# A four-layer graph network on one core: layers 1 and 2 worked by batches, biases by a row of ones, a shorter norm, and a counting ladder in PSUM

## The chip, the core and the metric

The kernel runs on one core of a Trainium2 chip. The metric is the device time of one execution in microseconds (us); lower is better. The engines are TensorE (PE; its weight loads are listed as PEld), VectorE (DVE), ScalarE (ACT), GpSimd (POOL) and SyncE (SP). POOL here issues all indirect DMAs (gathers, scatters and scatter-adds by index), SP and ACT the plain ones.

## What is computed

A graph of 3125 nodes with 64 features and 100000 edges, sorted by destination, goes through four layers. Each is `x = x + layer(relu(layernorm(x)))`, the norm without gain and bias.

```python
edge_index = jnp.stack([src, dst])
h = jnp.maximum(_layernorm(x, axis=-1), 0.0)
x = x + _L0_gnn_ref(h, edge_index, edge_weight, edge_weight_n2, ...)   # signed similarity, sums over dst and src
h = jnp.maximum(_layernorm(x, axis=-1), 0.0)
x = x + _L1_gnn_ref(h, edge_index, edge_type_8, ...)                   # 8 relations of attention
h = jnp.maximum(_layernorm(x, axis=-1), 0.0)
x = x + _L2_gnn_ref(h, src, dst, ...)                                  # gated messages, sum and max
h = jnp.maximum(_layernorm(x, axis=-1), 0.0)
x = x + _L3_gnn_ref(h, edge_index, ...)                                # 4 heads, batch norms, MLP
```

In layer 1 a node gets, besides the sum over its edges, its own row: `x @ W_self + b_self`, and for each relation r `alpha_self[r] * (h @ W[r]) + bias[r]` (the self loop). In layer 2 an edge takes `relu([h[src], h[dst]] @ We1 + be1)`, which the kernel splits in two tables: one row for the source and one for the destination, the latter with the bias `be1`.

## The kernel before

The nodes lie on 125 partitions with 25 tiles of 64 features each (`xn` is x, `hn` the normed h, `agg` what was collected, all 128x25x64 float32); node work goes in NBATCH = 5 batches of NB = 5 tiles. The edges lie on 128 partitions with 784 columns in 98 groups of 8. The five engines run their own hand-written programs and meet by counting semaphores; each takes its instructions strictly in the order in which they are written. The arena is one large SBUF tile whose parts have many names in the code.

**Layer 0.** POOL adds 784 columns of edge weights one by one into a table in DRAM, `weights0` (`add0`, line 707), in 14 windows of 56 columns. Beside this DVE merges equal keys (`merge_window`), norms x (`norm_relu(0)`), makes tables, and counts the edges of each node: `one_hot` (line 1536) compares, for a group of 8 columns, the row 0, 1, 2, ... (`iota_row`, the ladder, an SBUF tile) with the place of each edge, once 8x128 and once 8x25 wide, into bfloat16 ones and zeros; PE multiplies these (line 1118) and DVE adds the 25 counts (line 1529). That is 98 rounds. Then 32 tiles are weighed and summed (`weigh0`, `bend0`, `similarity0`, lines 1615, 1625 and 1633), each as soon as SP could load its cells (line 547), which waits for all windows of adds that the tile needs. The last three tiles need the last window.

**Between layers 1 and 2.** When the states of the edges are in DRAM (`state1`), POOL runs `whole_segments` and then `collect` twice (line 694): 25 gathers of `betas` (16 numbers a node) into `beta_n`, and 25 gathers of `state1` into `agg`. All count up one semaphore, `agg_in`; in the first collection POOL waits after each five until these have landed. DVE's `nodes1b` takes a batch: two small instructions on `beta_n`, then the products of PE (`mix`, line 1066: 5 narrow ones with `W_self`, 5 wide ones with the eight relations) in two parts, tiles 0 to 2 and 3 to 4 (`parts`). In a part DVE multiplies by the weights (line 1864, out of PSUM), sums over the eight relations with a reduction over a strided view (line 1866) and adds to `xn` (line 1868); the first part also adds the own product and the bias row (lines 1862 and 1863). Only when all five batches and all 25 gathers of `state1` are done, DVE adds `agg` to all of `xn` (line 1872), runs `norm_relu(2)` over all 25 tiles (lines 1477 to 1487; ACT takes the root, line 831), and begins `nodes2`.

**`nodes2`** goes by batches: DVE stages five tiles of `hn` (line 1492), PE transposes them (line 1052), ACT copies the result to `hT` (line 840), PE multiplies (line 1066, 5 products of 256 columns), and DVE copies one half to `tb2` (line 1883), `hn` beside it (line 1884), and the other half plus the bias `be1` to `bn_rows` (line 1886). SP stores `tb2` (line 581). After each batch POOL scatters its five tiles of `bn_rows` to `put2` (`put`, line 663); after the last it waits until they have landed, does `hold` (line 668), and begins the 784 gathers of layer 2 (`gather`, line 674).

## Time and profile before

| | us |
|---|---|
| median of 3 runs | 5234.94 |
| lowest and highest | 5234.36, 5235.63 |
| the profiled execution | 5238.84 |
| its span, in which all rows are placed | 5236.9 |

All starts and stretches below are in us from the start of that span. The profiled execution is 3.9 us above the median; 1.9 us of it lie around the span. The page puts DVE at 75% busy, POOL at 68%, PE at 54% and ACT at 15%: no engine is busy throughout, so what counts is who is waited for in each stage. A row of a timeline has the start, the busy time, engine, line, operation, output and inputs, how many, and in brackets the idle time before it with what ended it. A row of a grouped list has count, total busy time and mean of one, then the idle time of the engine just before.

### The profile page before, as it was taken

The page shows a single profiled execution, that of the slowest core. Times are in us where ns is not written, and L with a number is a line of the kernel's source. Part 1 is how long each engine was busy: PE and PEld are TensorE (multiplying, and loading weights), DVE is VectorE, ACT ScalarE, POOL GpSimd, SP SyncE. Part 2 cuts the span into 40 slices and gives each one's busy share as a digit, 9 for nine tenths or more (in the row PEclk, how much of TensorE's full clock was granted, in tenths as well). Part 3 has the DMA queues.
Part 4 walks back from the last instruction along what each step waited for, and adds up shares of the span by engine and source line. Part 5 has one row for each costly group of instructions (what it writes and reads, how often), then busy time and mean ns, then how long its engine had stood idle before and what let it go on. Part 6 is the DMA issues. An engine that isn't in the chain of part 4 may idle for free.

```text
span 5236.9 us, 62187 instructions
## 1 busy us (share of the span) xinstructions
PE 2819.4 (54%) x10695; PEld 1383.4 (26%) x10695; DVE 3951.2 (75%) x10482; ACT 777.7 (15%) x1979; POOL 3567.1 (68%) x3644
## 2 busy tenths in 40 slices
PE   5844277326675000014555555555777777738993
PEld 4522122104665000012222222222333333313332
DVE  8866999436999986655777777744888888889993
ACT  0000032110000025530222222210000000003331
POOL 4777777753777877755777777754777777725552
PEclk9999987657999555556777777667999999969996
DMA  9320266313444368852556656635999999938990
GB/s 348 139 89 9 76 228 225 126 63 123 165 159 159 122 234 301 298 182 88 182 179 183 181 180 179 182 96 204 307 309 313 308 311 308 311 123 285 332 324 21
DMA packets 458404, 1041.74 MB, mean 199 GB/s; under 512 B 129581, under 2 KB 247829, under 8 KB 427884
## 3 DMA queue, kind: packets, MB, share of 16 engines
q1 hardware_dynamic: 167018, 580.42, 30.8%
q0 software_dynamic: 131968, 217.09, 15.0%
q10 hardware_dynamic: 159234, 242.47, 13.3%
q14 instruction: 154, 1.26, 0.1%
q8 instruction: 30, 0.49, 0.0%
HBM read 560.07 MB, written 477.20 MB: 198 GB/s over the span
## 4 chain that ended last, share of the span: by engine, by line
POOL 43%; issue 20%; PE 16%; DVE 11%; DMA 7%; ACT 1%; DVEq 1%; POOLq 0%; ACTq 0%; SPq 0%
POOL arena L674 25%; POOL weights L707 16%; PE psum L1232 5%; PE psum L1233 4%; DMA arena<-tab,ring 4%; PE psum L1283 3%; DVE arena L2086 1%; DVE arena L1574 1%; DVE arena L1833 1%; PE psum L1066 1%; POOL agg L694 1%; DVE arena L2015 1%; POOL arena L694 1%; ACT arena L962 1%; DVE arena L1921 1%
## 5 line engine op out<-in xcount | busy, mean ns | idle before, releaser
L674 POOL DMA_INDIRECT arena<-tab,ring x2352 | 2313.4, 984 | 717.4 <-issue 697.0
L1232 PE MATMUL psum<-arena,ident 128*128 128x512 f32 x1176 | 791.3, 762 | 720.9 <-DMA arena<-tab,ring 537.2
L1574 DVE SCALAR_TENSOR_TENSOR arena<-arena,ns 128x64 f32<-128x64 f32 (+2 forms) x2351 | 870.1, 370 | 274.4 <-issue 74.8
L707 POOL DMA_INDIRECT weights<-arena x784 | 832.1, 1061 | 293.0 <-issue 238.7
L1233 PE MATMUL psum<-arena,ident 128*128 128x512 f32 x1176 | 723.0, 702 | 0.0
L1232 PEld LDWEIGHTS psum<-arena,ident 128*128 128x128 f32 x1176 | 265.0, 241 | 1142.7 <-issue 606.3
L777 POOL TENSOR_TENSOR arena<-arena,score 128x256 f32<-128x256 f32 x294 | 230.6, 809 | 256.8 <-issue 123.0
L1283 PE MATMUL psum<-arena,ident 128*128 128x512 f32 x784 | 362.8, 609 | 63.9 <-DVE arena L2086 63.8
L2015 DVE SCALAR_TENSOR_TENSOR arena<-psum,rowb 128x1024 f32<-128x1024 f32 x196 | 239.1, 1220 | 197.6 <-PE psum L1233 196.9
L1233 PEld LDWEIGHTS psum<-arena,ident 128*128 128x128 f32 x1176 | 271.7, 231 | 382.5 <-issue 382.5
L1154 PE MATMUL psum<-arena 64*128 64x400 f32 x512 | 159.4, 709 | 273.1 <-DVE arena L1633 265.1
L1200 PE MATMUL psum<-agg,arena 128*128 128x200 bf16 x2352 | 236.7, 250 | 118.7 <-DVE arena L1691 118.0
L1700 DVE SCALAR_TENSOR_TENSOR arena<-iota_row,base,psum 128x200 f32<-128x200 f32 x784 | 283.1, 417 | 1.6 <-PE psum L1200 1.6
L2086 DVE TENSOR_TENSOR arena<-arena,score 128x256 f32<-128x256 f32 x490 | 244.7, 538 | 28.0 <-PE psum L1283 27.9
L2022 DVE TENSOR_REDUCE arena<-arena 128x8 f32<-128x512 f32 x392 | 265.0, 677 | 0.1
L1900 DVE SCALAR_TENSOR_TENSOR arena<-psum,rowb 128x1024 f32<-128x1024 f32 x98 | 119.8, 1223 | 179.5 <-PE psum L1233 179.5
L1406 DVE SCALAR_TENSOR_TENSOR arena<-psum,arena,upper 128x128 bf16<-128x128 f32 x784 | 227.5, 348 | 30.6 <-PE psum L1023 30.1
L1083 PE MATMUL psum<-ident,arena 128*64 128x128 f32 (+1 forms) x3 | 1.2, 405 | 460.7 <-DVEq L1745 452.4
L1615 DVE SCALAR_TENSOR_TENSOR arena<-arena,limit 128x800 f32<-128x800 f32 x128 | 133.6, 1044 | 143.0 <-DMA arena<-weights 143.0
L1200 PEld LDWEIGHTS psum<-agg,arena 128*128 128x128 bf16 x2352 | 191.4, 98 | 152.1 <-DVE arena L1700 80.1
L897 ACT ACTIVATE arena<-arena,score 128x64 f32<-128x64 f32 x784 | 197.6, 334 | 211.2 <-DVE arena L1574 150.1
L1921 DVE SCALAR_TENSOR_TENSOR arena<-arena,ns 128x64 f32<-128x64 f32 x783 | 217.6, 278 | 6.3 <-ACT arena L962 4.8
(388 smaller groups left out, 4152.3 us busy)
## 6 DMA issues: line engine op xcount, KB each, us to landing
put<-zero SPq DMA_DIRECT2D x98, 1040.0 KB
arena<-put SPq DMA_DIRECT2D x98, 1040.0 KB, 7.5
spill<-arena ACTq DMA_DIRECT2D x98, 1024.0 KB, 5.4
arena<-spill SPq DMA_DIRECT2D x98, 1024.0 KB
state<-arena ACTq DMA_DIRECT2D x147, 512.0 KB, 3.6
weights<-zero SPq DMA_DIRECT2D x32, 1600.0 KB, 18.3
arena<-weights SPq DMA_DIRECT2D x32, 1600.0 KB, 7.5
put<-zero SPq DMA_DIRECT2D x14, 3584.0 KB
```

What stands on the lines that cost most here:

```text
L674: pool.indirect_dma_start(out=rows[:, h, k, :], out_offset=None, in_=table[:, :], in_offset=bass.IndirectOffsetOnAxis(ap=ring[:, h, word + ...
L707: pool.indirect_dma_start(out=weights0[:, :], out_offset=bass.IndirectOffsetOnAxis(ap=words0[:, g, k:k + 1], axis=0), in_=words0f[:, g, K ...
L1200: mm = pe.matmul(bank(2 + 2 * h + k // 2)[:, k % 2 * NT * R:(k % 2 + 1) * NT * R], lhsT=picks[:, h, k, :], rhs=s_parts[:, a, :], start=(a ...
L1232: pe.matmul(place, lhsT=ident[:, :], rhs=rows_of[0][:, s, columns, 0:width], start=True, stop=False)
L1233: mm = pe.matmul(place, lhsT=ident[:, :], rhs=rows_of[1][:, s, columns, 0:width], start=False, stop=True)
L1283: mm = pe.matmul(bank(h).rearrange("p (c k) -> p k c", k=K), lhsT=ident[:, :], rhs=y3[:, h, :, head * D:(head + 1) * D], start=(head == 0) ...
L1574: beats.add(dve.scalar_tensor_tensor(out=rows[:, s, k, :], in0=before, scalar=mark(ns, g, k), in1=rows[:, s, k, :], op0=ALU.mult, op1=ALU. ...
L1700: pick = dve.scalar_tensor_tensor(out=sifted[:, h * 4 + k, :], in0=iota_row[:, :], scalar=src_column[:, column], in1=bank(2 + 2 * h + k // ...
L1921: scans2.add(dve.scalar_tensor_tensor(out=st2[:, h, k, 0:D], in0=zero[:, 0:D] if start else prior[:, 0:D], scalar=mark(ns, g, k), in1=m2[: ...
L2015: beats3.add(dve.scalar_tensor_tensor(out=pr3[:, columns, :], in0=bank(4 * h + 2 * part, 2).rearrange("p (k c) -> p k c", c=HD), scalar=0. ...
L2022: beats3.add(dve.tensor_reduce(rs3[:, columns, :], pr3[:, columns, :].rearrange("p k (h c) -> p k h c", c=D), AX.X, ALU.add))
L2086: makes3.add(dve.tensor_tensor(y3[:, s % 2, k, :].rearrange("p (h c) -> p h c", c=D), gc3[:, s, k, 0:HD].rearrange("p (h c) -> p h c", c=D ...
```

## The change

1. **The counting ladder.** DVE copies the first 128 numbers of `iota_row` to PSUM bank 7 once, and `one_hot` reads them there. Its output and other input stay in SBUF.
2. **The norm.** The mean's scaling goes into the subtraction, epsilon and the scaling of the variance into ACT's root (bias and scale), and the relu into the last multiplication: eight DVE instructions become six.
3. **Biases.** A row of ones is added to `hT` (65th row), and `b_self` plus the eight relation biases, and `be1`, are written to the 65th row of the weights. The additions of the biases in `nodes1b` and `nodes2` go. The eight additions that form the bias go from between layers 1 and 2 to layer 0, before the weighing.
4. **Collecting.** POOL issues the 50 gathers of both collections one after the other; each batch has its own semaphore (`loops_in`, `arrived`).
5. **The sum over relations** is three additions (of 4, 2 and 1 rows) in place of the strided reduction.
6. **Add, norm and multiply by batches.** DVE adds `agg`, norms and stages a batch (`arrive1`) before the products of the batch ahead of it are copied out. ACT takes part in copying: tiles 2 and 3 (`ends2`), DVE the others.
7. Loops over the batches are written out, and some semaphores (`rows_in`, `kept`) are shared between stages with higher counts.

The core of the diff:

```diff
+            tally.done(pool.memset(hT_full[D:D + 1, :, :], 1.0), consts)
+            def collect_batches(table, index, rows, landed):
+                for i in range(NT):
+                    pool.indirect_dma_start(out=rows[:, i, :], out_offset=None, in_=table[:, :],
+                                            in_offset=bass.IndirectOffsetOnAxis(ap=index[:, i:i + 1], axis=0)).then_inc(landed[i // NB], 16)
-            collect(1, betas, eidx, beta_n, before=0)
-            ready((agg_in, 16 * NT))
-            collect(1, state1, eidx, agg)
+            collect_batches(betas, eidx, beta_n, loops_in)
+            collect_batches(state1, eidx, agg, arrived)
...
-                ready((taken, 15 + b + 1))
+                ready((rows_up, b + 1), (taken, 15 + b + 1))
...
-            deviation(2)
-            lift_only(3)
+            def ends2(b):
+                act.wait_ge(mixed, 15 + b + 1)
+                act.wait_ge(tab_out, b * 16 + 16 * (1 + 1 * NBATCH))
+                halves = bank(1).rearrange("p (j c) -> p j c", c=2 * HID)
+                act.activation(bn_rows[:, bass.ds(b * NB + 2, 2), :], halves[:, :, HID:2 * HID], ACT.Copy)
+                act.activation(tb2[:, 2:4, 0:HID], halves[:, :, 0:HID], ACT.Copy).then_inc(rows_up, 1)
+            for b in range(NBATCH):
+                deviation_of(2 + b, b)
+                if b:
+                    ends2(b - 1)
+                lift(3, b)
+            ends2(NBATCH - 1)
...
+            ladder = bank(7)[:, 0:P]
+            step(dve.tensor_copy(ladder, iota_row[:, 0:P]))
-                    dve.tensor_tensor(hots[:, h * K:h * K + K, :], spread(iota_row[:, 0:width].unsqueeze(1), P, K, width),
+                    dve.tensor_tensor(hots[:, h * K:h * K + K, :], spread(ladder[:, 0:width].unsqueeze(1), P, K, width),
...
+            def norm_batch(use, b):
+                at = bass.ds(b * NB, NB)
+                col = [lnv[:, k, at] for k in range(4)]
+                step(dve.tensor_reduce(col[0], xn[:, at, :], AX.X, ALU.add))
+                step(dve.scalar_tensor_tensor(out=hn[:, at, :], in0=spread(col[0].unsqueeze(2), P, NB, D), scalar=-1.0 / D, in1=xn[:, at, :],
+                                              op0=ALU.mult, op1=ALU.add))
+                step(dve.tensor_tensor(agg[:, at, :], hn[:, at, :], hn[:, at, :], ALU.mult))
+                step(dve.tensor_reduce(col[1], agg[:, at, :], AX.X, ALU.add))
+                dve.sem_inc(root_in, 1)
+                dve.wait_ge(root_out, use + 1)
+                step(dve.reciprocal(col[3], col[2]))
+                step(dve.scalar_tensor_tensor(out=hn[:, at, :], in0=hn[:, at, :], scalar=0.0, in1=spread(col[3].unsqueeze(2), P, NB, D),
+                                              op0=ALU.max, op1=ALU.mult))
...
-                        beats1n.done(dve.tensor_tensor(xn[:, at, :], xn[:, at, :], spread(row["b_self"].unsqueeze(1), P, NB, D), ALU.add))
-                    beats1n.done(dve.tensor_reduce(red1[:, lo:hi, :], prod1[:, lo:hi, :, :].rearrange("p j r c -> p j c r"), AX.X, ALU.add))
+                    for rows in (4, 2):
+                        beats1n.done(dve.tensor_tensor(prod1[:, lo:hi, 0:rows, :], prod1[:, lo:hi, 0:rows, :], prod1[:, lo:hi, rows:2 * rows, :], ALU.add))
+                    beats1n.done(dve.tensor_tensor(red1[:, lo:hi, :], prod1[:, lo:hi, 0, :], prod1[:, lo:hi, 1, :], ALU.add))
...
-            step(dve.tensor_tensor(xn[:, :, :], xn[:, :, :], agg[:, :, :], ALU.add))
-            norm_relu(2)
+            def arrive1(b):
+                at = bass.ds(b * NB, NB)
+                dve.wait_ge(arrived[b], 16 * NB)
+                step(dve.tensor_tensor(xn[:, at, :], xn[:, at, :], agg[:, at, :], ALU.add))
+                norm_batch(2 + b, b)
+                stage(3, b, hn)
...
+            arrive1(0)
+            for b in range(NBATCH):
+                if b < NBATCH - 1:
+                    arrive1(b + 1)
+                nodes2(b)
```

POOL's program at the two collections, from the end of `whole_segments` to the first scatter of layer 2; before:

```order
L694 DMA arena<-betas,eidx 128x16 [waits open_moved,beta_out]
L694 DMA arena<-betas,eidx 128x16 x4
L694 DMA arena<-betas,eidx 128x16 [waits agg_in]
L694 DMA arena<-betas,eidx 128x16 x4
...
L694 DMA agg<-state,eidx 128x64 [waits agg_in]
L694 DMA agg<-state,eidx 128x64 x24
L663 DMA put<-arena,zidx 103552x128 [waits taken]
```

and now:

```order
L695 DMA arena<-betas,eidx 128x16 [waits open_moved,beta_out]
L695 DMA arena<-betas,eidx 128x16 x24
L695 DMA agg<-state,eidx 128x64 x25
L667 DMA put<-arena,zidx 103552x128 [waits rows_up,taken]
L667 DMA put<-arena,zidx 103552x128 x4
```

The five waits of POOL on landed gathers are gone, and the scatter waits for two semaphores in place of one.

DVE's program from the end of `nodes1b` to the first copies of layer 2, where `lnv` holds the sums and roots of the norm and `hst` the staged batch; before:

```order
L1872 TENSOR_TENSOR xn<-xn,agg 128x1600 [waits agg_in,taken]
L1477 TENSOR_REDUCE lnv<-xn 128x25 [waits vec]
L1478 TENSOR_SCALAR lnv<-lnv 128x25 [waits vec]
L1479 TENSOR_TENSOR hn<-xn,lnv 128x1600 [waits vec]
L1480 TENSOR_TENSOR agg<-hn 128x1600 [waits vec]
L1481 TENSOR_REDUCE lnv<-agg 128x25 [waits vec]
L1482 TENSOR_SCALAR lnv<-lnv 128x25 [waits vec]
L1485 RECIPROCAL lnv<-lnv 128x25 [waits vec,root_out]
L1486 TENSOR_TENSOR hn<-hn,lnv 128x1600 [waits vec]
L1487 TENSOR_SCALAR hn<-hn 128x1600 [waits vec]
L1492 TENSOR_SCALAR hst<-hn 128x320 [waits turned,vec]
...
L1883 COPY arena<-psum 128x5x128 [waits tab_out,mixed]
```

and now:

```order
L1933 TENSOR_TENSOR xn<-xn,agg 128x320 [waits arrived0,taken]
L1520 TENSOR_REDUCE lnv<-xn 128x5 [waits vec]
L1521 SCALAR_TENSOR_TENSOR hn<-lnv,xn 128x320 [waits vec]
L1523 TENSOR_TENSOR agg<-hn 128x320 [waits vec]
L1524 TENSOR_REDUCE lnv<-agg 128x5 [waits vec]
L1527 RECIPROCAL lnv<-lnv 128x5 [waits vec,root_out]
L1528 SCALAR_TENSOR_TENSOR hn<-hn,lnv 128x320 [waits vec]
L1534 TENSOR_SCALAR hst<-hn 128x320 [waits turned,vec]
L1933 TENSOR_TENSOR xn<-xn,agg 128x320 [waits arrived1]
...
L1940 TENSOR_SCALAR arena<-hn 128x5x64 [waits tab_out]
L1945 COPY arena<-psum 128x256 [waits mixed,node_vec3]
```

Eight instructions on 320 columns now stand between `nodes1b` and the first staged batch, and the same eight for batch 1 stand ahead of the copies of batch 0.

## Rows read from the trace of the kernel before

**Rows 1.** The page's part 4: the chain that ended last, by line.

```profile
POOL arena L674 25%; POOL weights L707 16%; PE psum L1232 5%; PE psum L1233 4%; DMA arena<-tab,ring 4%; PE psum L1283 3%; DVE arena L2086 1%; DVE arena L1574 1%; DVE arena L1833 1%; PE psum L1066 1%; POOL agg L694 1%; DVE arena L2015 1%; POOL arena L694 1%; ACT arena L962 1%; DVE arena L1921 1%
```

**Rows 2.** Groups by line and shape, window 500 to 632, then 30 to 333, then 632 to 1143.

```profile
L1536 DVE TENSOR_TENSOR arena<-iota_row,arena 128x1024 bf16<-128x1024 f32 x81 | 98.2, 1212 | 0.0
L707 POOL DMA_INDIRECT weights<-arena x82 | 98.0, 1196 | 25.0 <-issue 25.0
...
L707 POOL DMA_INDIRECT weights<-arena x215 | 206.4, 960 | 119.5 <-issue 65.3 <-DVE arena L1428 54.3
...
L707 POOL DMA_INDIRECT weights<-arena x368 | 402.0, 1092 | 112.2 <-issue 112.2
...
L1615 DVE SCALAR_TENSOR_TENSOR arena<-arena,limit 128x800 f32<-128x800 f32 x116 | 121.1, 1044 | 93.7 <-DMA arena<-weights 93.7
```

**Rows 3.** Timeline around 540, DVE and POOL, two rounds of the counting.

```profile
540.14 1.49 DVE L1536 TENSOR_TENSOR arena<-iota_row,arena 128x1024 bf16<-128x1024 f32 x2
...
540.99 1.20 POOL L707 DMA_INDIRECT weights<-arena  x1 [0.30 <-issue]
```

**Rows 4.** Stretch 475 to 622: busy us (x instructions) of each engine, PEclk, DMA share, GB/s.

```profile
475.00:622.00 147.00, 38.34 (x784) 28.53 (x784) 146.53 (x294) 0.00 (x0) 117.24 (x98) 1.00 0.02 2
```

**Rows 5.** Timeline around 707, DVE and POOL, in the weighing of tiles.

```profile
706.74 0.99 DVE L1633 TENSOR_TENSOR arena<-arena,psum 128x800 f32<-128x800 f32 x1
706.85 0.96 POOL L707 DMA_INDIRECT weights<-arena  x1 [0.30 <-issue]
707.64 1.05 DVE L1615 SCALAR_TENSOR_TENSOR arena<-arena,limit 128x800 f32<-128x800 f32 x1
...
708.12 1.40 POOL L707 DMA_INDIRECT weights<-arena  x1 [0.30 <-issue]
```

**Rows 6.** Timeline: the last scatter-add, and the first weighing after it.

```profile
1142.63 0.96 POOL L707 DMA_INDIRECT weights<-arena  x1 [0.30 <-issue]
...
1152.02 1.05 DVE L1615 SCALAR_TENSOR_TENSOR arena<-arena,limit 128x800 f32<-128x800 f32 x1 [49.31 <-DMA arena<-weights]
```

**Rows 7.** Timeline, POOL's collections: first gather, first after a wait, last.

```profile
2326.81 0.96 POOL L694 DMA_INDIRECT arena<-betas,eidx  x1 [2.11 <-DMA state<-open_sum,open_end]
...
2334.86 0.95 POOL L694 DMA_INDIRECT arena<-betas,eidx  x1 [2.10 <-DMA arena<-betas,eidx]
...
2397.37 0.94 POOL L694 DMA_INDIRECT agg<-state,eidx  x1 [0.30 <-issue]
```

**Rows 8.** Timeline, DVE in `nodes1b`, first part of batch 1.

```profile
2348.51 0.49 DVE L1862 TENSOR_TENSOR xn<-xn,psum 128x320 f32 x1 [3.31 <-PE psum L1066]
2349.03 0.49 DVE L1863 TENSOR_TENSOR xn<-xn,rowb 128x320 f32 x1
...
2351.35 2.73 DVE L1866 TENSOR_REDUCE arena<-arena 128x192 f32<-128x1536 f32 x1
```

**Rows 9.** Timeline, DVE from the collected sums to the staged batch.

```profile
2399.86 1.83 DVE L1872 TENSOR_TENSOR xn<-xn,agg 128x1600 f32<-128x1600 f32 x1 [4.03 <-DMA agg<-state,eidx]
...
2409.36 0.18 DVE L1482 TENSOR_SCALAR lnv<-lnv 128x25 f32<-128x25 f32 x1
2409.89 0.31 DVE L1485 RECIPROCAL lnv<-lnv 128x25 f32<-128x25 f32 x1 [0.35 <-ACT lnv L831]
...
2413.12 0.33 DVE L1492 TENSOR_SCALAR hst<-hn 128x320 f32<-128x320 f32 x1
```

**Rows 10.** Timeline, batches of `nodes2`: PE, DVE, and POOL's scatters.

```profile
2415.62 4.50 PE L1066 MATMUL psum<-we_sb,hT 128*128 128x256 f32 x10 [0.79 <-ACT hT L840]
...
2420.16 0.82 DVE L1883 COPY arena<-psum 128x640 f32<-128x640 f32 x1 [4.96 <-PE psum L1066]
...
2423.10 1.00 POOL L663 DMA_INDIRECT put<-arena,zidx  x1 [24.78 <-DVE arena L1886]
...
2453.45 0.96 POOL L663 DMA_INDIRECT put<-arena,zidx  x1 [0.30 <-issue]
```

**Rows 11.** Timeline, DVE: the relu of the norm at layers 1 and 3.

```profile
1222.51 0.99 DVE L1487 TENSOR_SCALAR hn<-hn 128x1600 f32<-128x1600 f32 x1
...
3552.50 0.99 DVE L1487 TENSOR_SCALAR hn<-hn 128x1600 f32<-128x1600 f32 x1
```

More of the change, by code:

```diff
@@ L364, in gnn_program @@
         agg_in = sem("agg_in")
+        loops_in, arrived = ([sem(f"{name}{b}") for b in range(NBATCH)] for name in ("loops_in", "arrived"))
+        rows_up = sem("rows_up")
         result_out = sem("result_out")
@@ L1608, in _ @@
                 tally.done(dve.tensor_reduce(folded[:, :, :], prod.rearrange("p a (h c) -> p a h c", c=D), AX.X, ALU.add), wa_set)
+            dve.wait_ge(consts, 20)
+            for r in range(R):
+                step(dve.tensor_tensor(row["b_self"], row["b_self"], row["bias_rel"][:, r * D:(r + 1) * D], ALU.add))
+            for weights, bias in ((wself_full[D:D + 1, :], row["b_self"][D:D + 1, :]), (we1_full[D:D + 1, 1, :], row["be1"][D:D + 1, :])):
+                tally.done(dve.tensor_copy(weights, bias), wa_set)
             def weigh0(at, c):
@@ L1846, in _ @@
             dve.sem_inc(ended, 1)
-            for r in range(R):
-                step(dve.tensor_tensor(row["b_self"], row["b_self"], row["bias_rel"][:, r * D:(r + 1) * D], ALU.add))
-            beats1n = Beats(dve, node_vec[2], 8)
+            beats1n = Beats(dve, node_vec[2], 11)
             def nodes1b(b):
```

102 lines of the change are left out of this document (58 added, 44 removed).

## The prediction

> **What bounds the kernel now.** I read the chain that ended last first, since no engine is busy throughout. By line it belongs above all to POOL: 25% of the span are gathers of line 674 and 16% the scatter-adds of line 707 [rows 1]. The change touches neither loop of gathers, so I looked at the two places where it meets the chain: the scatter-adds, which run until 1143, and the stretch between layers 1 and 2, from 2327 to about 2455. For each I read the groups of instructions by stage and then the timeline.
>
> **Scatter-adds.** POOL waits there for nothing but its own issue, 0.30 us apiece, so its time per add is the length of the issue. Undisturbed one lasts 0.96 us (215 of them before 333), but 1.20 while DVE counts, and 1.09 on average while tiles are weighed [rows 2]. The timeline tells why. In the weighing, line 1615 reads two operands in SBUF: it ran from 707.64 to 708.69, and the add that began at 708.12 ended at 709.52, 0.83 after it. An add beside line 1633, whose second operand is in PSUM, took its 0.96 [rows 5]. In the counting DVE's line 1536 also reads two SBUF operands and the add that began at 540.99 took 1.20 [rows 3]: the 1024-wide comparison of 1.21 us began at 540.14 and ended at 541.35, and the add ended 0.84 after it. The two loops are locked: in 147 us there are 294 instructions of DVE (98 rounds of three) and just 98 issues of POOL, 1.50 us each [rows 4]. DVE itself is busy all the time and is not slowed.
>
> **Between the layers.** POOL begins the collections at 2326.81, waits after each five gathers (8.05 us for five), and issues the last at 2397.37 [rows 7]. DVE had sat idle for 4.03 us when that had landed; then it adds and norms all 25 tiles, from 2399.86 to 2413.12 [rows 9]. PE's first products last from 2415.62 to 2420.1, and POOL, idle for 24.78 us, begins to scatter at 2423.10. Its 25 scatters then follow one another: the last is at 2453.45, so 24 steps are 30.35 us, 1.26 each, with no room between [rows 10]. DVE's and PE's later batches are hidden behind them. So what counts is when the first scatter can start, and whether the others can still follow at 1.26.
>
> **The change, part by part.**
>
> *Ladder in PSUM.* The comparison then has one operand in SBUF, as line 1633 has, and an add beside it should take 0.96, so that 98 issues cost 1.26 in place of 1.50: 98 x 0.24 = **23.5 us**. What is late next? DVE keeps its 147 us for the counting (a comparison of PSUM with SBUF costs per element what one of two SBUF tiles costs: 0.99 us for 800, where 1024 of the present kind take 1.21, both 1.2 ns each [rows 2, 5]), so it is DVE that ends the counting, and POOL leaves it with 19 more adds done. The adds in the weighing are still stretched: 368 x 0.13 = 48 us for 116 instructions of line 1615, 0.41 each [rows 2], and these tiles are the same after the change. When the last add was out, DVE had been idle for 49.31 us [rows 6]; a last add 23.5 earlier finds it idle still. The eight bias additions and two copies now ahead of the weighing (some 2.5 us of DVE) fall into the same idle time. The lower bound is zero, if the stall has another cause; the upper is about 28, should the stretching in the weighing fall by a tenth with another phase.
>
> *Collections without waits.* 50 x 1.25 = 62.5 us from 2326.81: the last issue is at 2388.1 and has landed near 2391, 9 us earlier. DVE's new additions of two SBUF operands will stretch some of these issues. By the same reckoning a DVE instruction of length L costs a chance issue L x L / 2.5: 0.4 for the widest (below, 0.98), some 0.8 a batch in all, 4 us. That puts the last landing near 2395, which the norm of batch 4 needs only at about 2415. Hidden.
>
> *Sum over relations, and bias.* First part of a batch: the bias addition goes (0.52), and the reduction (2.76 with its gap [rows 8]) becomes additions of 768, 384 and 192 numbers. An addition takes 1.05 ns a number and 0.17 with its gap (0.49 for 320 and 1.83 for 1600 [rows 8, 9]): 0.98 + 0.57 + 0.37 = 1.92. Saved: 0.84 + 0.52 = 1.36. PE's next products start only when DVE has released the part, and DVE waits for them (3.31 us in batch 1), so this saving lies on the cycle of every batch: 5 x 1.36 = 6.8. The second part (1024 columns) saves 0.4 once, at the end. DVE was done 4.03 us before 2399.86, at 2395.8; now at 2388.6, and 2388.9 with some delay by POOL.
>
> *Norm by batches.* On 320 columns: four instructions of 0.51 (add, reduce, square, reduce), two of 0.53, 0.38 for ACT's root and 0.2 for the reciprocal: 3.7 us, where all 25 tiles took 13.3. Staged at 2392.6. From there as before: 2.5 to the products (2413.12 to 2415.62), 4.5 for them, and then four copies of DVE from PSUM with ACT's two beside them, 1.4 in place of 2.1, and 0.85 until POOL's scatter: 2.3. First scatter: 2392.6 + 2.5 + 4.5 + 2.3 = 2401.9, against 2423.10: **-21.2 us**.
>
> *Do the others follow?* DVE's cycle is now 4.0 (norm and staging of the next batch) + 0.45 (`hn` beside) + 1.4 (copies) = 5.9, with some delay by POOL 6.2, against 6.3 for five scatters. DVE's four instructions with two SBUF operands stretch POOL's issues by 4 x 0.1 a batch over four batches: +1.7. A PE that takes 4.5 for each batch is still ahead of DVE, since it works during the norm. So the last scatter comes at 2401.9 + 30.4 + 1.7 = 2434.0, **-19.4 us**. Bounds: -23 if PE's products run at their faster pace and nothing is stretched; -14 if DVE's cycle is 8 us, so that it, not POOL, sets the pace (2401.9 + 4 x 8 + 5.1 = 2439).
>
> *Shorter norm.* Two small instructions of 0.18 (0.22 and 0.27 with gap and signal) and the relu (1.03) go, and two instructions grow by 0.05: 1.4 us. In layers 1 and 3 nothing runs beside it [rows 11]: **2 x 1.4 = 2.8 us**. In layer 0 it is hidden by the adds.
>
> *At nothing:* loops written out, semaphores shared (each wait has its old meaning), the row of ones (one more memset of POOL, in the 54.3 us in which its first add waits for DVE [rows 2]). Between zero and 1 us either way.
>
> **Sum:** 23.5 + 19.4 + 2.8 = 45.7. Against the profiled execution, 5238.8 - 45.7 = 5193.1; the median lies 3.9 lower, so I forecast **5189** for it.
>
> **A rule of the Trainium skill.** The rows say that an add waits for a DVE instruction with two SBUF operands and not for one with an operand in PSUM. "SBUF — State Buffer", section "Who interferes with whom", has a rule for this (a DVE instruction with two SBUF inputs contends with a GpSimd instruction that reads SBUF), and by it the whole 23.5 us come. The same section infers that `tensor_tensor` does not hold up descriptors, as writing these needs the write interface; by that sentence the ladder's move would bring nothing. Rows 5 speak for the first.
>
> **Rivals.**
> *Ladder for nothing.* The comparison would still hold POOL, by its other operand or its bfloat16 output. For it: no row shows this very instruction with a PSUM operand. Against it: lines 1633 and 1615 differ in just that [rows 5]. Then the sum is 22.2: 5213. Chance 0.08.
> *DVE sets the pace of the scatters.* Each batch of DVE's has some 13 small instructions with waits between, two handovers to ACT, and POOL in its way. With a cycle of 8 us the time is 5 more: 5194. Chance 0.15.
> *Slower than before: reading the ladder from PSUM is slow.* A row of 128 numbers is read eight times over, 98 times. If a round took x us longer, DVE would begin the weighing 98x later. It idles there for 93.7 us before 1143 and for 49.3 at the end [rows 2, 6], 143 in all, of which POOL's lead takes 23.5; so up to x = 1.2 nothing is lost. From there DVE ends the layer, and the time is 5235 - 22 - 143 + 98x: above 5235 from x = 1.7, more than a doubled round, and 5286 at x = 2.2. The rows of line 1633 give x near 0. Chance 0.01.
> *Lead lost.* Something else than POOL ends layer 0 some 10 us later than I think, or a stage after it gives time back: 5199. Chance 0.06.
>
> **How the numbers follow.** Forecast as it stands, within some 3 us: 0.70, at 5189. The range of 8 in 10 takes in the slower pace, the lost lead and the upper ends (28, 23 and 3 make 54, which is 5181): 5181 to 5203. Beyond it lie the ladder for nothing and the slow ladder. A measurement of this kernel can tell about 0.2% (10 us) from no change. Every case but the slow ladder is faster by more than that: faster 0.97, same 0.02, slower 0.01.
>
> **What would show it.** Right: the adds of line 707 during the counting near 0.96 with more than 110 issues in the stretch; the last add near 1119; a first scatter of layer 2 some 21 us, and a last one some 19 us, earlier relative to the first gather of `betas`; the distance of scatters 1.26 to 1.35. Wrong: adds of 1.20 beside the counting; counting rounds longer than 1.5; gaps of DVE in POOL's scatters; DVE no longer idle before the last tiles of layer 0.

## The result, and the profile after

| | before | changed |
|---|---|---|
| median of 4 runs each, us | 5234.65 (5233.18 to 5235.63) | 5184.68 (5178.88 to 5186.93) |
| ratio to before | 1 | 0.9903 (95%: 0.9886 to 0.9920) |
| profiled execution, its span, us | 5238.84, 5236.9 | 5185.38, 5183.7 |
| last scatter-add, us of the span | 1142.63 | 1116.24 |
| first gather of `betas` | 2326.81 | 2298.14 |
| first, last scatter between layers 1 and 2 | 2423.10, 2453.45 | 2370.57, 2401.59 |

The changed kernel is 50 us (0.97%) faster. The forecast was 5189 us in a range from 5181 to 5203; the median lies 4.3 us below it, inside the range but outside the 3 us that I had given a chance of 0.70. The span is 53.2 us shorter, and the four places in the table divide it: 26.4 by the last add, 2.3 from there to the first gather, 23.2 between the layers, and 1.3 behind them.

**The counting.** The timeline of the changed kernel around 537 (columns as in [rows 3]), then its groups by line and shape in the window 500 to 632, as in [rows 2], and its stretch 475 to 622, as in [rows 4]:

```profile
537.27 1.48 DVE L1582 TENSOR_TENSOR arena<-psum,arena 128x1024 bf16<-128x1024 f32 x2
537.40 0.96 POOL L717 DMA_INDIRECT weights<-arena  x1 [0.31 <-issue]
538.66 0.96 POOL L717 DMA_INDIRECT weights<-arena  x1 [0.30 <-issue]
```

```profile
L717 POOL DMA_INDIRECT weights<-arena x101 | 98.0, 971 | 30.8 <-issue 30.8
L1582 DVE TENSOR_TENSOR arena<-psum,arena 128x1024 bf16<-128x1024 f32 x80 | 97.1, 1214 | 0.0
```

```profile
475.00:622.00 147.00, 39.76 (x787) 29.74 (x783) 145.68 (x296) 0.00 (x0) 111.33 (x118) 1.00 0.03 2
```

The comparison now has PSUM as its first input and lasts what it lasted (1214 ns against 1212). An add that runs wholly beside it takes 0.96 where [rows 3] have 1.20. In the same 147 us DVE makes 296 instructions (294 before), and POOL 118 issues in place of 98: the lock of one issue to a round is gone. Seven issues of each count are not adds but gathers of `tab` (line 668, now 672), which the prediction had taken with the adds; they fell from 1196 to 952 ns each, so gathers are held up like adds.

**The last add** (as in [rows 6]): DVE still idles 47.37 us behind it for the next tile, so POOL, not DVE, ends layer 0.

```profile
1116.24 0.96 POOL L717 DMA_INDIRECT weights<-arena  x1 [0.31 <-issue]
...
1125.45 1.05 DVE L1666 SCALAR_TENSOR_TENSOR arena<-arena,limit 128x800 f32<-128x800 f32 x1 [47.37 <-DMA arena<-weights]
```

**Between the layers.** Timeline of DVE in `nodes1b`, first part of batch 0 ([rows 8] show batch 1, which now begins at 2318.10 and has the same instructions); the three additions that replace the reduction of 2.73 us take 2308.37 to 2310.38, and the bias addition behind line 1911 is gone:

```profile
2306.06 0.49 DVE L1911 TENSOR_TENSOR xn<-xn,psum 128x320 f32<-128x320 f32 x1
2306.58 1.76 DVE L1912 TENSOR_TENSOR arena<-psum,arena 128x1536 f32<-128x1536 f32 x1
2308.37 1.61 DVE L1915 TENSOR_TENSOR arena<-arena 128x768 f32<-128x768 f32 x2
2310.02 0.36 DVE L1916 TENSOR_TENSOR arena<-arena 128x192 f32<-128x192 f32 x1
```

Then the sum and norm of batch 0, its products and the scatters (answering to [rows 9, 10]; DVE, PE and POOL):

```profile
2357.25 0.49 DVE L1933 TENSOR_TENSOR xn<-xn,agg 128x320 f32<-128x320 f32 x1
...
2360.26 0.19 DVE L1527 RECIPROCAL lnv<-lnv 128x5 f32<-128x5 f32 x1 [0.42 <-ACT lnv L845]
...
2361.00 0.52 DVE L1534 TENSOR_SCALAR hst<-hn 128x320 f32<-128x320 f32 x1
...
2363.71 4.63 PE L1090 MATMUL psum<-we_sb,hT 128*128 128x256 f32 x10 [0.79 <-ACT hT L854]
...
2368.45 0.42 DVE L1945 COPY arena<-psum 128x256 f32<-128x256 f32 x1 [2.54 <-PE psum L1090]
...
2370.57 1.00 POOL L667 DMA_INDIRECT put<-arena,zidx  x1 [7.83 <-DVE arena L1949]
...
2401.59 0.96 POOL L667 DMA_INDIRECT put<-arena,zidx  x1 [0.30 <-issue]
```

From the addition to the staged batch it is 3.75 us, where all 25 tiles took 13.3 (the norm itself now has six DVE instructions where it had nine, not eight as said under "The change"). POOL waits 7.83 us for its first scatter in place of 24.78. The last gather is issued at 2361.68, after the norm of batch 0 has begun.

### The profile page after: what moved, and what is told of

Read it like the earlier page. It is cut to its first block, busy times and chain, and to the rows that moved or that the text cites. A ratio compares the mean times of both kernels' runs of the same rounds, so it can differ in the third digit from the quotient of the medians.

```text
span 5183.7 us, 62148 instructions
## 1 busy us (share of the span) xinstructions
PE 2812.5 (54%) x10695; PEld 1380.3 (27%) x10695; DVE 3938.8 (76%) x10527; ACT 782.5 (15%) x1993; POOL 3545.7 (68%) x3645
## 4 chain that ended last, share of the span: by engine, by line
POOL 50%; issue 21%; PE 13%; DVE 10%; DMA 5%; DVEq 1%; POOLq 1%; ACT 0%; ACTq 0%; SPq 0%
POOL arena L678 33%; POOL weights L717 16%; PE psum L1311 3%; PE psum L1260 3%; PE psum L1261 3%; DMA arena<-tab,ring 3%; PE psum L1090 2%; DVE arena L2152 1%; DVE arena L1884 1%; DVE arena L1620 1%; DVE arena L2081 1%; DVE arena L1769 1%; POOL agg L704 0%; DVE arena L2132 0%; POOL arena L704 0%
## 5 line engine op out<-in xcount | busy, mean ns | idle before, releaser
L717 POOL DMA_INDIRECT weights<-arena x784 | 807.0, 1029 | 292.7 <-issue 238.7
L1666 DVE SCALAR_TENSOR_TENSOR arena<-arena,limit 128x800 f32<-128x800 f32 x128 | 133.5, 1043 | 115.7 <-DMA arena<-weights 115.7
```

The lines of the kernel that those rows point to most:

```text
L717: pool.indirect_dma_start(out=weights0[:, :], out_offset=bass.IndirectOffsetOnAxis(ap=words0[:, g, k:k + 1], axis=0), in_=words0f[:, g, K ...
```

## The experiments

The theory on record with the runs (**A**): POOL's issue of an indirect DMA is held up while DVE runs an instruction with two operands in SBUF, and not while one of them is in PSUM; POOL's issues set the end of layer 0. The rival **B**: the comparison holds POOL anyway (by its bfloat16 output, or by what it is), and the gain comes from the layers behind. For the second half: what the batches of the norm are worth, against the cheaper sum and biases alone. Unless another is named, each experiment is compared with the kernel before on its own chip. On the chip of the first four runs that one takes 5246.64 us.

**1. The ladder alone.** The kernel before, with only this:

```diff
+            ladder = bank(7)[:, 0:P]
+            step(dve.tensor_copy(ladder, iota_row[:, 0:P]))
...
-spread(iota_row[:, 0:width].unsqueeze(1), P, K, width)
+spread(ladder[:, 0:width].unsqueeze(1), P, K, width)
```

> The kernel before with only the ladder of the counting in PSUM. Theory A (a scatter-add waits for a DVE instruction with two SBUF operands): adds beside the counting take 0.96 us, about 117 issues in 475 to 622 instead of 98, and the kernel is 23.4 us (0.45%) faster. Theory B (the gain before the last add comes from the shorter norm or from DVE's order): adds stay at 1.20 and the time within 5 us.

Measured: 5219.76 us, ratio 0.9949 (0.9932 to 0.9966), 26.9 us less. Its groups in the window 500 to 615:

```profile
L1539 DVE TENSOR_TENSOR arena<-psum,arena 128x1024 bf16<-128x1024 f32 x78 | 94.3, 1210 | 0.0
L707 POOL DMA_INDIRECT weights<-arena x89 | 85.2, 958 | 27.1 <-issue 27.1
```

One operand moved and nothing else, and the issue is 958 ns: A.

**2. The other operand.** The kernel before with the ladder left in SBUF and the places it is compared with in PSUM. This asks whether it is PSUM as the ladder's home that matters, or the number of operands in SBUF.

```diff
+            pn_up, im_up = bank(4, 2)[:, 0:T], bank(6, 2)[:, 0:T]
+            step(dve.tensor_copy(pn_up, pn))
+            step(dve.tensor_copy(im_up, im))
...
-for hots, place, width in ((hot_p, pn, P), (hot_i, im, NT)):
+for hots, place, width in ((hot_p, pn_up, P), (hot_i, im_up, NT)):
```

> The kernel before with the ladder left in SBUF, but the other operand, the places of the edges, copied to PSUM (four banks, two copies of 784 columns, some 2 us of DVE). Theory A1 (what counts is that one of two operands is not in SBUF, whichever): the same gain as with the ladder in PSUM, 20 to 24 us. Theory A2 (it is the ladder's read, the same 128 numbers eight times over, or the tile that all of them share): no gain, within 3 us.

Measured: 5223.15 us, ratio 0.9955 (0.9938 to 0.9972), 23.5 less. Window 500 to 615:

```profile
L1540 DVE TENSOR_TENSOR arena<-iota_row,psum 128x1024 bf16<-128x1024 f32 x77 | 92.9, 1206 | 0.0
L707 POOL DMA_INDIRECT weights<-arena x89 | 85.5, 961 | 27.1 <-issue 27.1
```

Either operand will do. The output is still bfloat16 in SBUF, so writing it is not what holds POOL here.

**3. The ladder back.** The changed kernel with line 1582 reading `iota_row` in SBUF again (the diff of experiment 1, backwards).

> The changed kernel with the ladder back in SBUF. Theory A: 23.4 us slower than the changed one, adds of 1.20 beside the counting, last add near 1140, some 26 us faster than the kernel before. Theory B: within 5 us of the changed kernel.

Measured: 5223.63 us, ratio 0.9953 (0.9936 to 0.9970), so 23.0 less than before without the ladder's move. Window 500 to 615:

```profile
L1580 DVE TENSOR_TENSOR arena<-iota_row,arena 128x1024 bf16<-128x1024 f32 x78 | 94.5, 1212 | 0.0
L717 POOL DMA_INDIRECT weights<-arena x71 | 85.0, 1198 | 21.6 <-issue 21.6
```

The issue is at 1198 ns again. The two parts, 26.9 alone and 23.0 without, add up to 49.9, nearly the 50.0 of the whole change (each within some 9 us). So nothing shows that they share a gain or take one from each other.

The traces are sharper than the times. From the first add to the last it is 1080.42 us before (62.21 to 1142.63), 1054.84 with the ladder alone, 1078.61 with everything but the ladder, and 1053.61 in the changed kernel. So the ladder takes 25.6 or 25.0 us off this stretch, and all the rest of the change 1.8 or 1.2.

**4. The shorter norm alone**, in the kernel before:

```diff
-act.activation(lnv[:, 2, :], lnv[:, 1, :], ACT.Sqrt).then_inc(root_out, 1)
+act.activation(lnv[:, 2, :], lnv[:, 1, :], ACT.Sqrt, bias=sc[:, 13:14], scale=1.0 / D).then_inc(root_out, 1)
```

with the changed `norm_relu`.

> The kernel before with only the shorter norm, all four of them over 25 tiles. Theory as predicted (layer 0's norm is hidden by the adds): three norms of 1.4 us on the path, 4.2 us. Theory after the trace: in layer 0 the relu of 0.99 us and its neighbours also hold POOL, whose excess beside that norm fell from 10.3 to 7.6 us; so 4.2 + 2.7 = 6.9 us.

Measured: 5239.58 us, ratio 0.9985 (0.9976 to 0.9995), 7.1 less, with an interval from 2.6 to 12.6 us. That can't tell 4.2 from 6.9, so the time decides nothing between the two theories; the traces have to. The last add comes at 1137.77, 4.9 earlier than before, but 2.6 of that lie in the weighing, which this edit does not touch. The prediction had put the norm of layer 0 at nothing. It isn't quite, and the timeline of POOL there says why. First three rows of before, then of the changed kernel, which answer to each other:

```profile
390.01 2.36 POOL L707 DMA_INDIRECT weights<-arena  x1 [0.30 <-issue]
392.68 1.56 POOL L707 DMA_INDIRECT weights<-arena  x1 [0.30 <-issue]
...
397.06 2.08 POOL L707 DMA_INDIRECT weights<-arena  x1 [0.30 <-issue]
```

```profile
390.45 1.76 POOL L717 DMA_INDIRECT weights<-arena  x1 [0.30 <-issue]
392.51 1.55 POOL L717 DMA_INDIRECT weights<-arena  x1 [0.31 <-issue]
...
396.89 1.64 POOL L717 DMA_INDIRECT weights<-arena  x1 [0.30 <-issue]
```

Beside them DVE runs, in the kernel before,

```profile
389.72 1.82 DVE L1479 TENSOR_TENSOR hn<-xn,lnv 128x1600 f32<-128x1600 f32 x1
391.57 1.83 DVE L1480 TENSOR_TENSOR agg<-hn 128x1600 f32<-128x1600 f32 x1
...
396.17 1.82 DVE L1486 TENSOR_TENSOR hn<-hn,lnv 128x1600 f32<-128x1600 f32 x1
```

Each reads two operands in SBUF (line 1480 the same one twice). The add of 390.01 ended at 392.37, 0.83 after line 1479, and that of 392.68 at 394.24, 0.84 after line 1480. The third ended at 399.14, 1.15 after line 1486 but 0.13 after the relu that follows it (line 1487, 398.02 to 399.01), which is gone in the changed kernel; there the third ends 0.84 after the instruction beside it. So theory A reaches layer 0's norm too. But two operands in SBUF are not needed: the relu, with one, holds POOL as well. The kernels of experiments 1 and 2 still have it, and there this add again takes 2.08 us and ends 0.12 after it; in the kernel of this experiment, which is without it, the add takes 1.63:

```profile
397.62 1.63 POOL L707 DMA_INDIRECT weights<-arena  x1 [0.30 <-issue]
```

The reductions of lines 1477 and 1481 on as many numbers hold nothing: the adds that begin beside them take 0.96. The three adds together exceed three times 0.956 by 3.1, 3.2 and 2.5 us in the kernels with the old norm (before, experiments 1 and 2) and by 2.1, 2.2 and 2.5 in those with the new one (changed, experiments 3 and 4), as it falls out with the moment at which they begin. The norm of layer 0 is thus worth about 1 us (1.05 between the kernel before and the changed one).

**5. Sum and norm of layer 1 on all tiles at once.** The changed kernel, with the norm in one piece behind the last gather (ScalarE's root likewise once) and everything else as changed:

```diff
-                at = bass.ds(b * NB, NB)
-                dve.wait_ge(arrived[b], 16 * NB)
-                step(dve.tensor_tensor(xn[:, at, :], xn[:, at, :], agg[:, at, :], ALU.add))
-                norm_batch(2 + b, b)
+                if b == 0:
+                    for landed in arrived:
+                        dve.wait_ge(landed, 16 * NB)
+                    step(dve.tensor_tensor(xn[:, :, :], xn[:, :, :], agg[:, :, :], ALU.add))
+                    norm_relu(2)
```

> The changed kernel with the sum and the norm of layer 1 on all 20 tiles at once, after the last gather has landed, in place of batch by batch beside the gathers. Theory A (what the batches gain is that only a fifth of the sum and the norm is left behind the last landing): the first scatter between layers 1 and 2 is issued 10 to 12 us later than the 72.5 us after the first gather of betas that the changed kernel shows, the last one 9 to 11 us later, and the time is 5194 to 5197 us, 0.7 to 0.8% faster than before. Rival (the gain is in the sum of eight rows and in the biases alone, since the chain behind the last landing is the same sequence of waits between DVE and ScalarE whether it works on four tiles or on twenty): under 5 us later, 5185 to 5190 us.

Measured: 5208.01 us beside a kernel before at 5245.95 on that chip, ratio 0.9929 (0.9912 to 0.9946). The changed kernel's own ratio is 0.0026 lower, 13.6 us, within some 13 either way; the stretch itself is told by the trace. (The expectation speaks of 20 tiles; there are 25.) From the first gather of `betas` to the first scatter it is 87.1 us, where the changed kernel has 72.4: 14.7 more; to the last scatter 14.1 more. Timeline of DVE:

```profile
2365.05 1.82 DVE L1935 TENSOR_TENSOR xn<-xn,agg 128x1600 f32<-128x1600 f32 x1 [6.28 <-DMA agg<-state,eidx]
...
2374.75 0.31 DVE L1513 RECIPROCAL lnv<-lnv 128x25 f32<-128x25 f32 x1 [0.44 <-ACT lnv L840]
...
2376.95 0.33 DVE L1535 TENSOR_SCALAR hst<-hn 128x320 f32<-128x320 f32 x1
```

The batches win, and by more than the 10 to 12 us expected. I had counted the length of the norm only: 11.90 from the addition to the staged tile against 3.75, 8.1 us. The whole norm also has to wait 6.28 us for the last landing, as DVE's `nodes1b` is now done sooner than the gathers. Together 14.4 of the 14.7.

The other 9.2 of the 23.9 us at the first scatter, which this kernel keeps, are not the cheaper `nodes1b`, since DVE waits here for the last landing, and longer than before (6.28 against 4.03 us). They are that landing itself: the addition starts 65.81 us after the first gather of `betas`, where it was 73.05 before, 7.2 less, since POOL issues the gathers without waits. The shorter norm gives 1.4 of the rest (11.90 against 13.26) and the products and copies 0.6. So one of two gains counts at a time: with the norm in one piece the gathers bound the first scatter, and with batches `nodes1b` does.

**6. Does the rule reach further?** If A holds, the weighing of line 1615 (1666 in the changed kernel), which still stretches POOL's adds, should be worth moving too, and layer 2's collection can go without waits as layer 1's does. The changed kernel with both (cut to the core; `nodes2b`'s loop and semaphores follow from it, and the weighing moves behind `bend0`, so the order of DVE's three instructions changes as well):

```diff
-                dve.scalar_tensor_tensor(out=cells[:, place, columns], in0=per_src[:, columns], scalar=limit[:, ORDER[at]:ORDER[at] + 1],
-                                         in1=cells[:, place, columns], op0=ALU.min, op1=ALU.mult).then_inc(weighted, 1)
+                dve.scalar_tensor_tensor(out=dots_of(c), in0=per_src[:, columns].rearrange("p (b n) -> p b n", b=2), scalar=limit[:, ORDER[at]:ORDER[at] + 1],
+                                         in1=dots_of(c), op0=ALU.min, op1=ALU.mult).then_inc(weighted, 1)
...
-            collect(2, state2, eidx, agg2, before=0)
+            collect_batches(state2, eidx, agg2, arrived)
```

> The changed kernel with two additions: in the loop over 29 halves of line 1615 the weighing now multiplies the similarities in PSUM where it multiplied a tile in SBUF, so that the instruction has one operand in SBUF in place of two; and layer 2's collection is issued without POOL's waits after each five gathers, as layer 1's is. Theory A (an instruction of DVE with two operands in SBUF holds up POOL's issue of an indirect DMA, one with a single operand there does not; POOL's issues are what the first 1140 us hang on): the excess of the issues over 0.956 us between 646 and 1080 us, some 46 us in the changed kernel, falls by most, the last add issued near 1075 in place of 1116; with the waits of layer 2 gone some 5 to 8 us more, 5135 to 5150 us where the kernel before takes 5235. Rival: the weighing becomes slower on a PSUM operand or waits for the matmuls, the last add stays within 5 us of 1116 and the time within 10 us of the changed kernel's 5185. Both should be 1.0% to 1.9% faster than the kernel before; theory A says 1.6% or more.

Measured: 5137.42 us beside 5245.95, ratio 0.9795 (0.9779 to 0.9812): twice the gain of the change itself. Groups in the weighing, first of the changed kernel (window 640 to 1120), then of this one (640 to 1080):

```profile
L717 POOL DMA_INDIRECT weights<-arena x342 | 373.8, 1093 | 104.3 <-issue 104.3
...
L1666 DVE SCALAR_TENSOR_TENSOR arena<-arena,limit 128x800 f32<-128x800 f32 x116 | 121.0, 1043 | 68.4 <-DMA arena<-weights 68.3
```

```profile
L717 POOL DMA_INDIRECT weights<-arena x342 | 328.5, 960 | 104.1 <-issue 104.1
...
L1665 DVE SCALAR_TENSOR_TENSOR psum<-arena,limit,psum 128x800 f32<-128x800 f32 x117 | 123.5, 1056 | 4.2
L1675 DVE SCALAR_TENSOR_TENSOR psum<-psum,sc,arena 128x800 f32<-128x800 f32 x117 | 123.3, 1054 | 23.2 <-ACT arena L877 23.1
```

The same 342 issues take 328.5 us in place of 373.8, and the last one begins at 1070.48 in place of 1116.24: 45.8 us. Not one of them takes more than 0.98 us, where 110 took more than 1.03 in the changed kernel, as theory A has it; the new order alone was not tried. DVE pays 13 ns an instruction; its wait of 23 us for ScalarE is not new (26.8 in the changed kernel), and its idle time for cells from DRAM falls from 68.3 to 47.3 us. In layer 2, from the first gather of the collection to the norm it is 41.45 us (3393.06 to 3434.51), where the changed kernel has 51.34 (3438.15 to 3489.49): 9.9 us. Both together make 55.7; the ratios 0.9795 and 0.9903 are 56.6 us apart, within some 13.

**Runs that decided nothing.** Six more were made, on two other chips: the waits of the first collection put back (twice), the reduction of eight rows put back, the norm in one piece, the weighing in PSUM, and experiment 6's kernel. On both chips every kernel took 7434 to 7732 us, the kernel before among them (7464.79 and 7472.51), with idle of the engines in the middle of their loops that the trace ascribes to "remote" or to its issue. Each with its expectation:

The waits of the first collection put back (`if held and i and i % NB == 0: ready(...)` in `collect_batches`): 7652.05 us.

> The changed kernel with the waits of POOL on each five gathers of betas, and on the last five before the gathers of state, put back. As predicted (hidden, since DVE's products end later than the gathers, and the last batch is needed only at its norm): within 1 us of the changed kernel up to the first scatter; the gathers end 9 us later, at 71 us from the first of them, where the first scatter came at 72.4, so that it is on the edge: 0 to 1.5 us slower. Rival (the gathers bound the stretch): 9 us slower.

The same once more, 7662.90 us:

> The changed kernel with the waits of POOL on each five gathers of betas, and on the last five before the gathers of state, put back. As predicted (hidden, since DVE's products end later than the gathers, and the last batch is needed only at its norm): the gathers end 9 us later, 71 us after the first of them, where the first scatter came at 72.4, so that it is on the edge: 0 to 1.5 us slower than the changed kernel. Rival (the gathers bound the stretch): 9 us slower.

The reduction of eight rows put back, 7699.12 us:

```diff
-                    for rows in (4, 2):
-                        beats1n.done(dve.tensor_tensor(prod1[:, lo:hi, 0:rows, :], prod1[:, lo:hi, 0:rows, :], prod1[:, lo:hi, rows:2 * rows, :], ALU.add))
-                    beats1n.done(dve.tensor_tensor(red1[:, lo:hi, :], prod1[:, lo:hi, 0, :], prod1[:, lo:hi, 1, :], ALU.add))
+                    beats1n.done(dve.tensor_reduce(red1[:, lo:hi, :], prod1[:, lo:hi, :, :].rearrange("p j r c -> p j c r"), AX.X, ALU.add))
```

> The changed kernel with the strided reduction over relations in place of the three additions. As predicted: 0.84 us on each of five batches and 0.4 at the end, 4.6 us slower, first scatter 4.6 later from the first gather. Rival (part of the gain is a higher granted clock of TensorE since its waits are shorter): 6 to 8 us slower, with products of 6.9 to 7.3 us in more batches.

The norm in one piece (experiment 5), 7707.66 us:

> The changed kernel with the sums added and normed over all 25 tiles at once before the first batch is staged, the rest unchanged. By the working: 13.3 - 1.4 = 11.8 us in place of 4.2 up to the staged batch, so the first scatter 7.6 later, plus up to 4 us of waiting for the last gather, which landed 66 us after the first one where DVE needs it at 59: 10 to 12 us later for the first scatter, and the last one 9 to 11 us later, since DVE's cycle is then shorter than five scatters. Rival (the scatters' pace hides it): under 5 us slower.

The weighing in PSUM without the freed collection (half of experiment 6), 7711.92 us:

> The changed kernel with the weighing by node norms (line 1615 of before, two SBUF operands) applied to the similarities in PSUM in place of the cells in SBUF; same work and order of tiles. Theory A: the adds from 646 on lose their stretching too, 45 us of excess over 0.956 fall to under 5, the last add comes near 1075, DVE still has idle time before the last tiles, and the kernel is 35 to 45 us faster than the changed one (5140 to 5150). Rival: DVE's three dependent instructions and the wait at the cells cost it as much as the lead, and the end of layer 0 moves by under 10 us.

Experiment 6's kernel, 7727.78 us:

> The changed kernel with two additions. First, the weighing by node norms (line 1615 of before, two SBUF operands) is applied to the similarities in PSUM in place of the cells in SBUF, same work and order of tiles. Theory A (an add waits for a DVE instruction with two SBUF operands): the excess of the adds over 0.956 us falls from 46 us to under 5 in the stretch from 646 on, the last add comes near 1075 in place of 1116, and layer 0 ends 35 to 42 us earlier. Rival: DVE's three dependent instructions cost it the lead, and the end of layer 0 moves by under 10. Second, POOL's second collection (layer 2, between the gathers of layers 2 and 3) goes without waits, each batch with its own semaphore: 4 to 8 us, since DVE waits there for each batch. Together 5150 to 5140 where the kernel before takes 5235, that is 1.7% faster than before.

None of these times can be set against 5185. Beside the kernel before on their own chip they are 2.6 to 3.5% slower (ratios 1.026 to 1.035), where on the chip of the experiments everything was faster than before; the changed kernel itself was not run there. So the gain of 0.97% is shown where the kernel before takes 5235 us, and what the change does on those chips is open. One row of the kernel with the reduction put back shows why even the single stretch is of no use there, DVE waiting ahead of a batch whose inputs had long been there:

```profile
4201.76 0.49 DVE L1911 TENSOR_TENSOR xn<-xn,psum 128x320 f32<-128x320 f32 x1 [19.55 <-remote]
4202.28 1.76 DVE L1912 TENSOR_TENSOR arena<-psum,arena 128x1536 f32<-128x1536 f32 x1
4204.08 2.73 DVE L1914 TENSOR_REDUCE arena<-arena 128x192 f32<-128x1536 f32 x1
```

What slows those chips is not known. The norm in one piece and experiment 6 were therefore run again. How the 9.9 us of `nodes1b` divide among the sum, the bias and the waits of POOL no undisturbed run shows; below they are read from the traces alone.

## Why the prediction was right

**Ladder (predicted 23.5).** Right in mechanism and size. In 475 to 622 the issues exceeded 0.956 us by 23.4 us in sum before and by 0.2 now. One more add, at 474.33, stood beside the first comparison and took 1.84, 0.9 too much. From first to last add the ladder gives 25.6 or 25.0 (experiment 3), and alone it measures 26.9, with an interval of about 9 either way. POOL made 20 more issues there (19 predicted), and the DVE round did not grow, as forecast. A lasting part of the stall is in the weighing: 1093 ns an add (forecast: as before, 1092).

**The norm of layer 0 ("hidden by the adds").** This step failed, if by little. I asked whether the adds hide DVE's time, and did not ask what DVE's instructions do to the adds, though I had just found that out for lines 1536 and 1615. The three adds shown in experiment 4 take 6.00 us together before and 4.95 now: 1.05 us. Over the whole stretch from 330 to 475 the excess of the issues falls by 2.7 us, from 10.3 to 7.6, and the expectation of experiment 4 put all of that down to the norm. It isn't: 0.9 are the add at 474.33, which is the ladder's, and 0.6 are an add beside line 1515, which the change doesn't touch (434.92, 3.77 us; now 434.17, 3.18 us) and which came at another moment. The last add comes 26.4 earlier where 23.5 was forecast: 24.1 from the counting, 1.05 from the norm, and 1.3 net from other places, where adds meet DVE's untouched instructions at another moment.

**Shorter norm in layers 1 and 3 (1.4 each).** Right. From the first reduction to the staged batch it was 11.41 us in layer 1 and is 10.05, and in layer 3 (with one small instruction between) 11.74 and 10.37. Between the last add and the first gather 2.3 us disappear; 0.8 of the remaining 0.9 lie ahead of the norm, in the end of layer 0. No term had them, and the same stretch differs by over 3 us among the kernels of the experiments (1181.97 to 1185.39), so nothing follows from it.

**Collections without waits ("hidden").** Right for the changed kernel, by its trace: the last gather is issued at 2361.68, and the addition of batch 4 needs it at 2381.2, 83.1 us after the first gather. At the pace of before, 70.56 us from first to last issue, it would still be there in time; no undisturbed run put the waits back. But it hides only because the norm is batched. In experiment 5, with the norm in one piece, DVE waits 6.28 us for that landing, and the freed gathers give 7.2 us.

**Sum over relations (1.36 a batch, 6.8 in all; 7.2 by the end of `nodes1b`).** The terms hold: 2.04 us for the three additions against the 1.92 of the sum, the bias addition gone. Yet `nodes1b` ends 9.9 us earlier relative to the first gather, where 6.9 were forecast with some delay by POOL: 3.0 more. What was left out is PE, whose products the sum took as they were. Timeline of PE, the products of two batches, before and changed:

```profile
2354.53 1.99 PE L1066 MATMUL psum<-wself_sb,hT 128*128 128x64 f32 x10 [3.91 <-DVE xn L1868]
2356.31 5.56 PE L1066 MATMUL psum<-wrel_sb,hT 128*128 128x512 f32 x10
...
2366.32 2.39 PE L1066 MATMUL psum<-wself_sb,hT 128*128 128x64 f32 x10 [3.90 <-DVE xn L1868]
2368.51 6.29 PE L1066 MATMUL psum<-wrel_sb,hT 128*128 128x512 f32 x10
```

```profile
2322.80 1.33 PE L1090 MATMUL psum<-wself_sb,hT 128*128 128x64 f32 x10 [2.55 <-DVE xn L1918]
2323.97 6.21 PE L1090 MATMUL psum<-wrel_sb,hT 128*128 128x512 f32 x10
...
2333.27 1.33 PE L1090 MATMUL psum<-wself_sb,hT 128*128 128x64 f32 x10 [2.55 <-DVE xn L1918]
2334.43 6.21 PE L1090 MATMUL psum<-wrel_sb,hT 128*128 128x512 f32 x10
```

Narrow and wide products go together. Those of batches 1 to 4 took 9.3, 7.3, 8.5 and 8.8 us before and take 8.9, 7.4, 7.4 and 7.3 now: 33.9 against 31.0, and DVE waits for them in every batch. These 2.9 us are nearly all of the 3.0. It is TensorE's clock that differs: it has two levels, 1.2 and 2.4 GHz, and its granted share is 0.77 over each batch that takes 7.3 to 7.4 us, and 0.60 to 0.66 over the others.

The same holds on the other undisturbed traces. In experiments 3, 5 and 6, which have the new `nodes1b`, PE idles 2.5 to 2.6 us ahead of batches 2 to 4 and takes 7.3 to 7.4 us for each, at 0.77. In experiments 1, 2 and 4, with the old one, it idles 3.9 to 4.0 us and the products of batches 2 and 3 take 8.7 to 9.0, at 0.62 to 0.65. One batch doesn't fit, the first one shown: it took 7.3 us at 0.77 behind 3.91 us of idle. So the shorter idle goes with the higher clock in all batches but that one; that it is the cause no run isolates, as the sum, the bias and POOL's waits changed together.

**Norm by batches and the first scatter (-21.2).** Measured -23.9, 2.7 more: the 3.0 just named, less 0.3 in the other steps, which are right nearly to the tenth: norm 3.75 (3.7), to the products 2.71 (2.5), products 4.63 (4.5), copies and POOL 2.23 (2.3).

**The other scatters.** 24 steps take 31.02 us, where 30.35 + 1.7 were forecast: DVE's two-operand instructions cost POOL 0.7, not 1.7. DVE's cycle is 5.8 us (its addition of line 1933 comes at 2369.64 for batch 2 and at 2381.2 for batch 4), where 5.9 to 6.2 were forecast, so the rival that DVE sets the pace falls. Last scatter: -23.2, forecast -19.4.

The terms give 45.7 by forecast and 53.2 in the trace. Of the 7.5 missed, 2.9 are in the adds (1.05 of them layer 0's norm), 0.9 between them and the gather, 3.8 between the layers (2.7 of them at the first scatter, which is PE), and -0.1 behind. The term that was most too small is thus what lies between the layers, 19.4 by forecast and 23.2 in the trace. That the median came nearer to the forecast than the profiled execution (4.3 us off, not 7.7) is luck: the latter lay 3.9 above the median before and 0.7 above it now. Of the rivals, "ladder for nothing" and "slower" fall by experiments 1 to 3, and "lead lost" by the last add, whose 26.4 us all arrive at the first gather of `betas`.

## What to carry to other kernels

Where POOL issues indirect DMAs back to back, look at what DVE runs beside them, not only at who waits for whom: there is no wait in the trace, only a longer issue. Moving one operand of the most frequent two-operand instruction to PSUM gave 0.5%, and of the next one, with a collection freed of its waits, 1.1% more. Before calling an edit hidden, ask what the instructions that it shortens do to the engine that hides them. And where a norm stands behind a collection, look at gathers and norm together: freeing the gathers alone brought the last landing 7.2 us forward, and cutting the norm into batches that follow the gathers gave its own length and the wait for that landing on top (8.1 and 6.3 us here).

## What the runs showed of the hardware

- An indirect DMA that begins while DVE runs an instruction with two SBUF operands ends 0.82 to 0.87 us after that instruction. This holds for `tensor_tensor` on 1024 (all 97 issues that begin in the stretch of the counting before, most at 1.20 us in place of 0.96) and on 1600 numbers (1.55 to 2.44), and for `scalar_tensor_tensor` on 800 (110 adds in the weighing before, 1.00 to 1.74). With these instructions it is the start of the issue that counts: 84 adds that began 0.31 us or more ahead of an instruction of line 1615 and ran into it took 0.95 to 0.96. With either operand in PSUM it is 958 to 961 ns. The Trainium skill's inference in "SBUF — State Buffer", "Who interferes with whom", that `tensor_tensor` doesn't hold up descriptors, doesn't hold here (experiments 1 to 3); its rule on two SBUF inputs does.
- An operand in PSUM costs DVE next to nothing in these shapes: 1214 against 1212 ns for 1024 numbers, 1056 against 1043 for 800 (experiment 6).
- The relu on 1600 numbers with one operand (0.99 us) holds an issue too: in three kernels the add that runs into it ends 0.12 to 0.13 us after it, and without the relu this add takes 1.63 in place of 2.08 us (experiment 4). A `tensor_reduce` on 1600 numbers with one operand does not (0.96 us).
- TensorE's granted clock over the counting was 0.50 (1.2 GHz) in the kernels of experiments 1 and 4, and 1.00 (2.4 GHz) in those of before, of experiments 2 and 3 and in the changed one. The counting took the same time in all, as DVE, with 146 of 147 us busy, sets its pace.
